# Window attention and a batch-norm convolution: four-column image shift moved into the transfers, V in two column halves, side taps in array quarters

## What is computed

```python
def _L0_conv_ref(x, qkv_w, proj_w, proj_b, bias_table):     # shifted window attention
    x = jnp.roll(x, (-SHIFT, -SHIFT), axis=(2, 3))          # SHIFT = 4, windows of 8 x 8
    qkv = jnp.einsum('bchw,oc->bohw', x, qkv_w)
    ...
    attn = jnp.einsum('wnqd,wnkd->wnqk', q, k) * SCALE      # 4 heads of 16, 64 positions per window
    attn = softmax(attn + bias + mask)
    out = jnp.einsum('wnqk,wnkd->wnqd', attn, v)
    ...
    out = jnp.einsum('bchw,oc->bohw', out, proj_w) + proj_b[None, :, None, None]
    return jnp.roll(out, (SHIFT, SHIFT), axis=(2, 3))

def _L1_conv_ref(x, gamma, beta, w_lbp, w_1x1, b_1x1):
    xn = batch_norm(x) * gamma + beta
    y = conv_3x3(xn, w_lbp)
    y = jax.nn.relu(y) + x
    return jnp.einsum('bohw,oc->bohw', y, w_1x1) + b_1x1

x = x + _L0_conv_ref(_ln_c(x), ...)                         # layer norm over the 64 channels
...
x = x + _L1_conv_ref(_ln_c(x), ...)
```

## Time and profile before

| | |
|---|---|
| timed runs, median (lowest to highest) | 6532.88 us (6526.73 to 6534.02), 3 runs |
| profiled execution | 6523.44 us |
| its span, first to last instruction | 6521.7 us |
| busy: TensorE, VectorE, ScalarE, GpSimd | 5177.3, 4375.0, 3663.2, 1265.4 us |
| attention stage, from the span's start | 0 to about 1141 us |
| convolution stage | about 1373 to 1953 us, its strips from 1555 us |

### The profile page before, as it was taken

The page is one execution under the profiler, slowest core; times in us unless marked ns, Lnnn a source line. Parts: engine busy times, 40 slices in busy tenths (PEclk is TensorE's granted clock), DMA queues, the critical chain, the costliest instruction groups (busy, mean ns, idle before and its releaser), DMA issues. The chain is left out here.

```text
span 6521.7 us, 132203 instructions
## 1 busy us (share of the span) xinstructions
PE 5177.3 (79%) x45758; PEld 3396.3 (52%) x45758; DVE 4375.0 (67%) x9710; ACT 3663.2 (56%) x6942; POOL 1265.4 (19%) x1164
## 2 busy tenths in 40 slices
PE   6886887636996888499969998605999999958887
PEld 4664665223542333299969997202555555523332
DVE  7886887875227888832223345878777777759886
ACT  5664666645436776532243322646766766646765
POOL 3443444043220000510000000032111111121110
PEclk9998999857998999599989999857999999979999
DMA  1111111422336888300000023335666666538776
GB/s 32 34 31 27 34 34 27 131 62 81 87 84 209 280 275 278 104 23 0 0 0 0 20 98 114 94 93 97 83 85 82 83 85 80 73 104 249 243 233 220
DMA packets 794230, 645.98 MB, mean 99 GB/s; under 512 B 496551, under 2 KB 644199, under 8 KB 793779
## 3 DMA queue, kind: packets, MB, share of 16 engines
q1 hardware_dynamic: 792755, 639.06, 39.4%
q0 software_dynamic: 1024, 1.05, 0.1%
HBM read 549.78 MB, written 90.20 MB: 98 GB/s over the span
## 5 line engine op out<-in xcount | busy, mean ns | idle before, releaser
L2343 PE MATMUL sw_pC<-sw_row,sw_wc 128*128 128x128 f32 x10160 | 1159.4, 274 | 56.2 <-DVE sw_row L2218 54.9
L2343 PEld LDWEIGHTS sw_pC<-sw_row,sw_wc 128*128 128x128 f32 x10160 | 1148.2, 191 | 58.2 <-DVE sw_row L2218 55.5
L2777 PE MATMUL sp_pC<-sp_work,sp_bands 64*64 64x512 f32 (+11 forms) x14592 | 985.7, 428 | 43.6 <-issue 43.6
L2206 DVE SCALAR_TENSOR_TENSOR sw_row<-sw_pC,sw_y 128x128 f32<-128x128 f32 x1016 | 337.1, 332 | 792.8 <-PE sw_pC L2343 792.8
L2777 PEld LDWEIGHTS sp_pC<-sp_work,sp_bands 64*64 64x64 f32 x14592 | 600.5, 133 | 432.0 <-issue 364.3
L2716 ACT ACTIVATE sp_pC<-sp_pC,sp_par 128x512 f32<-128x512 f32 x832 | 597.7, 740 | 371.6 <-PE sp_pC L2777 348.1
L1757 DVE TENSOR_TENSOR t_z<-t_z,t_ht 128x1024 f32<-128x1024 f32 x512 | 624.9, 1269 | 79.1 <-DMA t_z<-gate_rows 39.8
L1920 PE MATMUL t_pO<-t_z,t_ew 128*64 128x512 f32 x2048 | 527.3, 634 | 113.7 <-DVE t_z L1757 110.6
L2275 ACT ACTIVATE sw_y<-sw_row 128x128 f32 (+1 forms) x762 | 265.4, 348 | 593.2 <-DVE sw_row L2206 593.2
L2673 DVE TENSOR_TENSOR sp_work<-sp_work,sp_pC 128x512 f32<-128x512 f32 x512 | 351.3, 688 | 169.6 <-ACT sp_pC L2716 169.1
L308 POOL TENSOR_TENSOR wa_sc<-wa_sc,wa_sm 128x1024 f32<-128x1024 f32 x128 | 243.4, 1902 | 554.1 <-DVE wa_sm L404 554.1
(11 more groups left out here) (369 smaller groups left out, 10429.8 us busy)
## 6 DMA issues: line engine op xcount, KB each, us to landing
t_z<-gate_rows SPq DMA_DIRECT2D x512, 512.0 KB, 7.7
sp_bands<-windows SPq DMA_DIRECT2D x128, 512.0 KB
c_spent<-tokens SPq DMA_DIRECT2D x128, 256.0 KB, 2.6
cb_xs<-tokens SPq DMA_DIRECT2D x128, 256.0 KB, 2.8
wa_xs<-in_x SPq DMA_DIRECT2D x64, 256.0 KB, 2.8
tokens<-wa_xt SPq DMA_DIRECT2D x128, 128.0 KB, 2.3
tokens<-cb_h SPq DMA_DIRECT2D x64, 256.0 KB, 2.4
t_xs<-tokens SPq DMA_DIRECT2D x32, 512.0 KB, 10.2
```

Source lines behind the costliest of these rows:

```text
L2206: dve.scalar_tensor_tensor(row[par][c][:, :, PAD:PAD + P2], pC[c][:, 0:2 * P2].rearrange("p (b w) -> p b w", b=2), 0.0, line(sweep, c, i), ...
L2343: ins = pe.matmul(pC[c][:, 0:2 * P2], wc[:, sweep, m, :], row[1 - par][c][:, :, m:m + P2], start=(m == 0), stop=(m == 4))
L2777: ins = pe.matmul(out[halves[to], :, low * lo:low * hi], band[halves[k], (NV * g + j) % BANDS, q, AT[k][tap], :], v[halves[k], :, low * at ...
```

## The change

1. Attention: `load` fetches columns 4 to 127 and columns 0 to 3 as two transfers, so `xs` lies in shifted order; `store` writes partitions 0 to 123 and 124 to 127 as two transfers. `normalised` and `residual` become one instruction each.
2. Attention: `h` holds each window once; GpSimd's `write_h` is gone. V comes from two matmuls per window with 64 weight columns, one for each half of the output's partitions. On VectorE the save of V now stands ahead of the write of h in step 2.
3. Convolution: strips are worked in pairs. `straight` makes the three full matmuls of a strip (for odd strips with `w_crossed`, whose output halves are exchanged), `beside` the side taps of both strips as twelve matmuls of 64 x 64, each in one quarter of the array. Four PSUM banks (`pC` and `pH`) and four buffers of `xn` and `xb` are used, and the strips are written out in place of the loops. `add_relu` takes an odd strip in two halves.

```diff
-        h = a.sb("h", [128, 2, W // WS, 2, WS, WS])
+        h = a.sb("h", [128, 2, W // WS, WS, WS])
...
-        def normalised(eng, par, copy):
-            for w0, w1, c0, c1, col in ((0, 15, 0, WS, SHIFT), (15, 16, 0, 4, W - 4), (15, 16, 4, 8, 0)):
-                def part(t):
-                    return t[:, :, col:col + (w1 - w0) * (c1 - c0)].rearrange("p r (w c) -> p w r c", c=c1 - c0)
-                ins = eng.tensor_tensor(h[:, par, w0:w1, copy, :, c0:c1], part(xc), part(sq), ALU.mult)
-            return ins
+        def normalised(eng, par):
+            def part(t):
+                return t[:, :, :].rearrange("p r (w c) -> p w r c", c=WS)
+            return eng.tensor_tensor(h[:, par, :, :, :], part(xc), part(sq), ALU.mult)
...
-                    sp.dma_start(xs[:, k, 4 * half:4 * half + 4, :], src).then_inc(x_in[k], 16)
+                    rows = xs[:, k, 4 * half:4 * half + 4, :]
+                    sp.dma_start(rows[:, :, 0:W - SHIFT], src[:, :, SHIFT:W]).then_inc(x_in[k], 16)
+                    sp.dma_start(rows[:, :, W - SHIFT:W], src[:, :, 0:SHIFT]).then_inc(x_in[k], 16)
...
-                        rows = tok[bass.ds((2 * bp + g) * S + r * W, 4 * W), :]
-                        sp.dma_start(rows.rearrange("(r w) c -> w r c", r=4),
-                                     xt[:, par, 4 * half:4 * half + 4, 64 * g:64 * g + 64]).then_inc(stored[par], 16)
+                        rows = tok[bass.ds((2 * bp + g) * S + r * W, 4 * W), :].rearrange("(r w) c -> w r c", r=4)
+                        part = xt[:, par, 4 * half:4 * half + 4, 64 * g:64 * g + 64]
+                        sp.dma_start(rows[SHIFT:W], part[0:W - SHIFT]).then_inc(stored[par], 16)
+                        sp.dma_start(rows[0:SHIFT], part[W - SHIFT:W]).then_inc(stored[par], 16)
...
-            def write_h(m, par, done):
-                pool.wait_ge(rstd_ready, m + 1)
-                pool.wait_ge(qkv_ready, done + 1)
-                normalised(pool, par, 1).then_inc(h_doubled, 1)
...
-                pool.tensor_tensor(o[:, :, SHIFT:W], xs[:, k, :, SHIFT:W], p[:, :, 0:W - SHIFT], ALU.add)
-                pool.tensor_tensor(o[:, :, 0:SHIFT], xs[:, k, :, 0:SHIFT], p[:, :, W - SHIFT:W],
-                                   ALU.add).then_inc(x1_ready, 1)
+                pool.tensor_tensor(o, xs[:, k, :, :], p, ALU.add).then_inc(x1_ready, 1)
...
                     softmax_shift(s, j, last)
+                    if after:
+                        save_v(*after[0:2])
                     if j == 2 and not last:
                         write_h(n + 1, (k + 1) % 2, NSTEP * n)
-                    if after:
-                        save_v(*after[0:2])
...
-                    keys = ht[:, w, :, :].rearrange("p t q -> p (t q)")
-                    ins = pe.matmul(pV[:, w, :], keys, w_cols[:, 2, :], start=True, stop=True)
-                ins.then_inc(qkv_ready, 1)
+                    for copy in range(2):
+                        ins = pe.matmul(pV[64 * copy:64 * copy + 64, w, :], ht[:, w, :], w_cols[:, 2, :], start=True, stop=True)
+                        if w == STEP - 1:
+                            ins.then_inc(qkv_ready, 1)
...
+                if m == 0:
+                    other = slice(64 - 64 * po, 128 - 64 * po)
+                    ins = dve.tensor_copy(w_crossed[rows, :, other], w_tap[rows, tap:9:3, :])
...
+                if par == 0:
+                    ins = dve.scalar_tensor_tensor(out, p[:, :], 0.0, before, ALU.max, ALU.add)
+                else:
+                    for half in range(2):
+                        here, there = slice(64 * half, 64 * half + 64), slice(64 - 64 * half, 128 - 64 * half)
+                        ins = dve.scalar_tensor_tensor(out[here, :], p[there, :], 0.0, before[here, :], ALU.max, ALU.add)
...
-                for k in range(3):
-                    for beside, src in enumerate((xn, xb)):
-                        ins = pe.matmul(pC[par][:, :], wc[:, k, beside, :], src[:, par, k:k + R, :],
-                                        start=(k == 0 and not beside), stop=(k == 2 and beside == 1))
+            def straight(n):
+                pe.wait_ge(xn_ready, n + 1)
+                if n >= 4:
+                    pe.wait_ge(y_ready, n - 3)
+                for k in range(3):
+                    w = wc[:, k, 0, :] if n % 2 == 0 else w_crossed[:, k, :]
+                    ins = pe.matmul(banks[n % 4][:, :], w, xn[:, n % 4, k:k + R, :], start=(k == 0), stop=False,
+                                    skip_group_check=True)
+                ins.then_inc(straight_done, 1)
+            def beside(m):
+                pe.wait_ge(straight_done, 2 * m + 2)
+                for k in range(3):
+                    for n in (2 * m, 2 * m + 1):
+                        for pi in range(2):
+                            rows, cols = slice(64 * pi, 64 * pi + 64), slice(64 - 64 * pi, 128 - 64 * pi)
+                            to = cols if n % 2 == 0 else rows
+                            ins = pe.matmul(banks[n % 4][to, :], wc[rows, k, 1, cols], xb[rows, n % 4, k:k + R, :],
+                                            start=False, stop=(k == 2), skip_group_check=True)
+                            if k == 2:
+                                ins.then_inc(conv_ready, 1)
...
+            for m in range(B * NT // 2):
+                for par in range(2):
+                    straight(2 * m + par)
+                if m > 0:
+                    for par in range(2):
+                        mix(2 * m - 2 + par)
+                beside(m)
```

More of the change, by code:

```diff
@@ L284, in _ @@
             for par in range(2):
[L285 removed]
+                sp.wait_ge(stored[par], 128 * STRIPS + 16)
         @block.gpsimd
@@ L332, in body @@
                         residual(n - 1, (k - 1) % NX)
-                    if j == 2 and not last:
-                        write_h(n + 1, (k + 1) % 2, NSTEP * n)
                 steps(n, k, first, last, body)
@@ L1222, in _ @@
             link = Link(pool, pool_done)
-            for s in (var_ready, conv_ready, u_saved, y_ready):
+            for s in (var_ready, u_saved):
                 pool.sem_inc(s, 1)
@@ L1343, in add_rest @@
                                   xs[:, par, :, :].rearrange("p t c -> p (t c)"), pY[par][:, :], ALU.add).then_inc(sum_ready, 1)
-            def strip(b, i, n, par, top, bottom):
-                add_relu(b, i, n, par)
-                add_rest(n, par)
-            over_strips(dve, strip)
+            for n in range(0, B * NT, 2):
+                add_relu(n)
+                add_relu(n + 1)
+                add_rest(n)
+                add_rest(n + 1)
         @block.scalar
```

95 lines of the change are left out of this document (45 added, 50 removed).

## The result

The changed kernel takes **6440.87 us** (median of 4 runs, 6432.86 to 6443.21) where the kernel before takes 6530.86 beside it: ratio 0.986, 95% interval 0.9843 to 0.9877, 90 us faster. The forecast was 6416 in a range of 6396 to 6452. So it went the way that was said, and 27 us of the 117 that were added up did not come. The profiled execution took 6438.65 us, its span 6436.9, which is 84.8 less than the 6521.7 of before.

A forecast was written before the change was run, and what follows sets the result against it. TensorE bounds the convolution; in attention no engine is full, and VectorE's late write of h delays step 2. Profiled 6523.4 less 40 (attention) and 76.5 (convolution) gives 6407, or 6416 us as a median; range 6396 to 6452.

The forecast's parts named there:

- The convolution: Convolution strips: a pair takes 9.66 us against 12.08 with TensorE still full; 76.5 us gained in all.
- I add 0.14 for the change of form: Convolution, per pair of strips: TensorE's cost of switching to 64 x 64 matmuls, 0.14 us on top of 2.58.
- Attention's write of h: Attention, step 2: one VectorE instruction replaces three, ending the sum's delay behind the exponential; 48 us over 30 strips.
- So 1.6 us go per strip: Attention, step 2: the mean delay of the softmax sum behind the exponential vanishes, 1.6 us in each of 30 strips.
- V's save now comes first, inside the wait for the root: Attention, step 2 on VectorE: saving V during the wait lets h be ready about 1.25 us after the root.
- V in halves: Attention on TensorE: eight 64-column matmuls, two at once, take 1.00 us, 0.11 more; charged in two steps, 7 us loss.
- 1.1 + (1.6 + 1.1) + 1.6 = about 5.5 us loss: Attention's edges: extra load and store issues at the first load, the turn to the second image pair and the end.
- the rival of stores on few engines: Attention's 124-partition stores run on four DMA engines: about 8 us at the end, 4 at the turn; 6428 us, chance 0.27.
- Its sign: Four-engine stores would show as 8 to 10 us between the last store issue and the next stage's first load.
- No wait took the whole of attention's gain: Rival: in attention, V's pairs not overlapping or late scores eat the gain; about 6464 us, chance 0.10.
- quarters in one bank: Rival: convolution row halves sharing a PSUM bank run only two at once; side taps 5.16 us, total 6499, chance 0.03.
- stores never bound the strips: Rival: attention's 124-partition stores on one DMA engine need 40 us against a strip's 31; 6672 us, chance 0.04.

The follow-up runs named there:

- the quarters taken twice: Changed kernel with the convolution's 64 x 64 side-tap matmuls split into two places per pair, the first row tap between the two mixes: 6445.18 us, ratio 0.9884.
- the second profile: The changed kernel run again with no edit: 6439.26 us, ratio 0.9876 to the kernel before.
- the saves-first order: Step 2: TensorE's queries to values before variance, ScalarE's saves before logarithm and root. On the changed kernel 6381.88 us (0.978); on the kernel before 6514.78 us (0.9994).

## Why the prediction was right, and where it was not

**The convolution: right, one term too small.** But for the change of form, full matmuls, mixes and quarters took what the rows of before said; ScalarE, VectorE and TensorE's wait for its own full matmuls ahead of the quarters never held it. "I add 0.14 for the change of form" was the mis-sized term: it is 0.35, shown by the quarters taken twice. 32 x 0.21 = 6.7 us, against a shortfall of 5.8.

**Attention's write of h: the step is right, the sum too large.** The 1.6 us between exponential and sum are gone, and the two starts gained the 2.45 us each that were said (VectorE's write to TensorE's queries 3.74 us before, 1.28 after, at the first). But from one write of h to the next an ordinary strip went from 32.34 to 31.18 us (means of 24 strips of either profile), 1.16 in place of 1.6 less 0.22.

The missing part is TensorE's clock. In a few strips it keeps the full clock behind its wait for the logarithm, and there the sum holds: counted from wait to wait, such a strip takes 31.80 to 31.91 us before (four of them) and 30.46 after (four of them), 1.34 to 1.45 less. One of either kernel, before first:

```profile
286.46 1.09 PE L621 MATMUL wa_pL<-wa_sq,wa_mean_w 128*128 128x512 f32 x2 [2.85 <-ACT wa_sq L488]
...
318.26 1.38 PE L621 MATMUL wa_pL<-wa_sq,wa_mean_w 128*128 128x512 f32 x2 [2.85 <-ACT wa_sq L488]
```

```profile
645.00 1.10 PE L612 MATMUL wa_pL<-wa_sq,wa_mean_w 128*128 128x512 f32 x2 [2.85 <-ACT wa_sq L479]
...
675.45 1.10 PE L612 MATMUL wa_pL<-wa_sq,wa_mean_w 128*128 128x512 f32 x2 [2.84 <-ACT wa_sq L479]
```

In that strip of the changed kernel V is in time and the exponential ends 2.2 us after the root (651.40 and 649.19), where it was 2.2 to 2.6: what is late next is ScalarE's exponential, as said. In 26 of the 30 strips (22 in the second profile) variance, queries, keys or values are made at the lower clock. In the one shown above the exponential then waits for V and ends 2.9 us after the root. What failed is "So 1.6 us go per strip": the sum has no term for TensorE, which the step now waits for. The prediction read VectorE's and ScalarE's rows and not TensorE's wait for the logarithm and the clock behind it, though the waits of before have it too, 88.0 us in 32 strips.

The four strips behind a turn of the loop gained nothing where 1.38 us each were due: 137.6 us in all before, 140.5 and 137.8 in the two profiles of the changed kernel. There TensorE waits 2.3 to 3.4 us for its own instructions, and then gets the lower clock at some turns, in either kernel: at two of four before, at three and two in the two profiles after. Queries and keys behind the first turn after the change; before, behind the first and the third:

```profile
200.35 2.08 PE L553 MATMUL wa_pQK<-wa_h,wa_w_cols 128*128 128x256 f32 x4
```

```profile
205.52 1.13 PE L563 MATMUL wa_pQK<-wa_h,wa_w_cols 128*128 128x256 f32 x4
...
768.48 2.08 PE L563 MATMUL wa_pQK<-wa_h,wa_w_cols 128*128 128x256 f32 x4
```

Why some turns and strips get the lower clock and others not stays open. That the bound had moved on, and was not gone, is shown: the saves-first order is worth 57 us behind the change and some 6, if any, ahead of it.

**"V's save now comes first, inside the wait for the root": idle.** The old order gave the same time.

**V in halves: near.** 1.02 us from start to start at the full clock against 1.00 forecast, so two do run at once; not foreseen was that Q with K ahead of them took 1.06 instead of 0.97.

**The edges: the step that failed most.** "1.1 + (1.6 + 1.1) + 1.6 = about 5.5 us loss" counted issues alone. Measured: first load to TensorE's mean 1.8, turn 15.6 - 7.3 = 8.3, end 10.2 - 4.9 = 5.3, in all 15.4. Here the rival of stores on few engines, with 0.27, held in kind: its part is 5.9 us where 12 were priced. Its sign, 8 to 10 us behind the last store's issue, showed otherwise: 3.3 us, because SP had already waited inside its issues. Of the 20 us that attention fell short, 10 are the edges' and 10 the strips'.

**The other rivals.** No wait took the whole of attention's gain, though TensorE's took a part of it; quarters in one bank overlap; stores never bound the strips, as at the stage's end a strip's are through within 10.0 us (1112.76 to 1122.76) and a strip takes some 31.

**Other stages at nothing:** right within their spread of some 7 us.

**The range.** That 6440.87 us lies inside it is partly luck: its upper part was added up from a smaller gain per strip and from stores on few engines, while the 27 us that did not come are 10 of the strips, 10 of the edges and 6 of the convolution, only in part from those causes.

## What to carry to other kernels

When a stall is taken away, look for the next one on every engine that feeds the same step, TensorE's granted clock included: a wait of 2.85 us ahead of its matmuls was mostly paid twice here, and putting saves ahead of it brought more than the edit that exposed it. Edges of a stage (first load, turn, last store) have no cover, so count there what a transfer does on the engines and on its queue, not only its issue, and let the next round's loads go ahead of the last stores (tried here only together with two other edits). A shape that packs small matmuls pays a fixed price each time it is entered and left, so gather them.

## What the runs showed of the hardware

- Going into 64 x 64 quarters and out again cost 0.35 us, in a stage where TensorE was full at the full clock.
- Behind an idle time of 2.85 us TensorE went on at the lower clock for a while in 26 of 30 strips, and at the full one in 4 (22 and 8 in the second profile). In the strip shown 0.66 was granted, and work of 2.1 us took 3.6. Moving matmuls ahead of the wait changed which work was slow, and 12 of 30 strips kept the full clock.
- VectorE's subtraction of 1024 elements from two SBUF inputs takes 1.23 us in the first strip, and 2.93 in step 2 beside GpSimd's residual sum (2.87 in a strip of before). The Trainium skill, GPSIMD Engine Reference, Specifications, says that GpSimd shares its way to SBUF with VectorE and collides with instructions of two SBUF inputs; these rows agree. Nothing here tried to move the sum away.

```profile
410.58 2.34 POOL L315 TENSOR_TENSOR wa_x<-wa_xs,wa_yr 128x1024 f32<-128x1024 f32 x1
411.07 2.93 DVE L388 TENSOR_TENSOR wa_sc<-wa_sc,wa_mx 128x1024 f32<-128x1024 f32 x1
```

- A DMA issue on SP can take 0.26 us and hold the next one for 1.15: the small store's long issue was the large store's, since a piece of 4 partitions behind one of 12 takes 0.25.
